# A transformer block with modulation: prologue shared out among queues and engines, row maxima of the second item spread over its own attention, last item's tail reordered

## The reference

```
c6 = silu(c) @ Wc + bc
sh_msa, sc_msa, g_msa, sh_mlp, sc_mlp, g_mlp = split(c6, 6)
xm = ln(x) * (1 + sc_msa) + sh_msa
q, k, v = xm @ Wq + bq, xm @ Wk + bk, xm @ Wv + bv
w = softmax((q / 16) . k)            # per item and head, 512 x 512
x = x + g_msa * ((w . v) @ Wo + bo)
xm2 = ln(x) * (1 + sc_mlp) + sh_mlp
x = x + g_mlp * (gelu(xm2 @ W1 + b1) @ W2 + b2)
```

## Time and profile before

| | us |
|---|---|
| median of 3 runs | 711.07 (711.01 to 713.25) |
| profiled execution, its own time | 709.01 |
| its span, first to last instruction | 707.2 |
| PE busy in it | 672.8 (95%) |
| DVE busy | 552.4 (78%) |
| ACT busy | 398.5 (56%) |
| POOL busy | 238.0 (34%) |

### The profile page before, as it was taken

The page is one execution under the profiler, slowest core; times in us unless marked ns, Lnnn a source line. Parts: engine busy times, 40 slices in busy tenths (PEclk is TensorE's granted clock), DMA queues, the critical chain, the costliest instruction groups (busy, mean ns, idle before and its releaser), DMA issues.

```text
span 707.2 us, 15832 instructions
## 1 busy us (share of the span) xinstructions
PE 672.8 (95%) x6498; PEld 410.8 (58%) x6498; DVE 552.4 (78%) x1013; ACT 398.5 (56%) x474; POOL 238.0 (34%) x179
## 2 busy tenths in 40 slices
PE   7989998989999999999999999999999989999987
PEld 6543334323787448854687448844686437833976
DVE  5989989699877988789867988789867985742654
ACT  7545663466525874288525874288625871388231
POOL 1770015103442136212452136212452213250444
PEclk9999999999999999999999999999999998999999
DMA  9745105410453007230453107230452111011110
GB/s 305 212 105 131 57 32 161 112 62 33 126 132 103 35 33 194 50 120 31 103 155 99 40 32 192 51 121 32 117 141 65 44 34 61 32 61 63 47 38 30
DMA packets 58104, 63.57 MB, mean 90 GB/s; under 512 B 7560, under 2 KB 49054, under 8 KB 58030
## 3 DMA queue, kind: packets, MB, share of 16 engines
q1 hardware_dynamic: 58032, 62.56, 30.8%
HBM read 24.15 MB, written 12.89 MB: 52 GB/s over the span
## 4 chain that ended last, share of the span: by engine, by line
PE 75%; DVE 11%; issue 4%; DMA 3%; ACT 3%; SPq 2%; POOL 1%; ACTq 0%; DVEq 0%; POOLq 0%
PE ps L821 20%; PE ps L881 13%; PE ps L767 13%; PE ps L957 12%; PE ps L827 6%; DVE mx L1222 5%; PE ps L1036 3%; PE ps L813 2%; PE ps L918 2%; SPq L491 2%; PE ps L1043 2%; ACT prob L708 1%; PE ps L926 1%; DVE stats L1143 1%; DMA qst<-mrow 1%
## 5 line engine op out<-in xcount | busy, mean ns | idle before, releaser
L1222 DVE TENSOR_REDUCE mx<-ps 128x1 f32<-128x512 f32 x512 | 330.0, 682 | 49.0 <-PE ps L827 32.7
L708 ACT ACTIVATE prob<-ps 128x1024 f32<-128x1024 f32 x256 | 248.8, 1022 | 113.7 <-PE ps L821 65.3
L821 PE MATMUL ps<-qst,kst 98*32 98x512 bf16 x1920 | 142.6, 379 | 1.7 <-ACT prob L708 1.7
L881 PE MATMUL ps<-prob,vaug 128*32 128x512 f32 x1024 | 133.7, 594 | 1.2 <-DVE mx L1222 0.5
L821 PE MATMUL ps<-kst,qst 96*32 96x512 bf16 x1348 | 127.6, 381 | 4.8 <-DVE mx L1222 3.3
L646 POOL TENSOR_TENSOR hl<-z,hh 128x512 fp32r<-128x512 f32 x64 | 82.3, 1286 | 123.1 <-DVE hh L1417 123.1
L754 ACT ACTIVATE z<-ps,bias_t 128x512 f32<-128x512 f32 x64 | 43.8, 687 | 120.7 <-PE ps L957 115.8
L821 PEld LDWEIGHTS ps<-qst,kst 98*32 98x32 bf16 x1920 | 51.9, 96 | 68.7 <-issue 25.2
L821 PEld LDWEIGHTS ps<-kst,qst 96*32 96x32 bf16 x1348 | 37.1, 94 | 82.1 <-DVE mx L1222 47.7
L767 PE MATMUL ps<-w_hi,hh 128*128 128x256 f32 x256 | 73.8, 288 | 2.5 <-POOL hl L646 2.5
L827 PE MATMUL ps<-kst,qst 96*128 96x512 bf16 x201 | 66.2, 398 | 7.3 <-DVE mx L1222 6.4
(11 more groups left out here) (144 smaller groups left out, 927.5 us busy)
## 6 DMA issues: line engine op xcount, KB each, us to landing
qst<-prob SPq DMA_DIRECT2D x72, 128.0 KB, 3.5
kst<-prob SPq DMA_DIRECT2D x72, 128.0 KB, 3.8
y_scratch<-rb SPq DMA_DIRECT2D x28, 256.0 KB, 2.0
xd<-in_x_dram SPq DMA_DIRECT2D x8, 512.0 KB, 3.9
xa<-in_x_dram SPq DMA_DIRECT2D x7, 512.0 KB, 4.6
yc<-y_scratch SPq DMA_DIRECT2D x14, 256.0 KB
rb<-r_scratch SPq DMA_DIRECT2D x14, 256.0 KB
out_dram<-xn SPq DMA_DIRECT2D x7, 512.0 KB, 3.2
```

Of the source, the lines that this page charges most:

```text
L708: act.activation(prob[:, s % 2, 2 * p:2 * p + 2, :], ps[:, 2 * p:2 * p + 2, :], ACT.Exp, scale=1.0 / DH).then_inc(exp_done, 1)
L821: m = pe.matmul(out[32 * n:32 * n + 32, :], weights[:, 32 * n:32 * n + 32], moving, start=True, stop=True, skip_group_check=True)
L881: m = pe.matmul(ps[32 * q:32 * q + 32, 4 + g % 2, :], vaug[par][:, kt, G * g + q, :], prob[:, s % 2, q, :], start=kt == 0, stop=kt == TT - ...
L1222: dve.tensor_reduce(mx[(i + 1) % 2][:, t, h:h + 1], ps[:, BANK_OF[q], :], AXX, ALU.max).then_inc(max_done, 1)
```

## The change

The edits are of three kinds.

**Prologue.** Modulation is computed turned: Wc's blocks are the weights and silu(c) moves, so the features land on partitions and `turn_modulation` goes; only the two gates are still made as rows. bc comes in with the other biases, which PE turns before the modulation. The first columns of Wc are loaded from ACT's queue, and ACT loads its exponential table before it waits for c. ACT makes the high part of Wq and Wk, POOL the low part. POOL writes the keys' rows of -1 in two pieces. For item 0, ACT makes `zh` and DVE makes `z`, from opposite banks. Three of the twelve fills of item 0's first stack are issued from ACT's queue.

**Second attention.** Of item 1's 64 blocks, 46 instead of 56 lie ahead of its attention, and 18 instead of 8 in its first steps; of item 2's, 30 instead of 40 lie in that attention and 34 instead of 24 behind it. Item 1's maxima are turned in three groups (8, 4 and 4 heads) instead of two.

**Tail.** POOL adds one half of item 7's residual and DVE the other; DVE takes the low part of hidden tile 6, POOL's inverse root no longer stands ahead of it; item 7 is normalised behind hidden tile 7; DVE and ACT share its modulation; item 6's output sum stands behind hidden tile 1 of item 7; item 7 leaves in pieces of 2, 1 and 1 token tiles.

```diff
 C_FIRST = {
     0: ((4,) * 9 + (3,) + (0,) * 6, (0,) * 9 + (1,) + (4,) * 6),
-    1: ((0, 0, 0, 0, 4, 4) + (0,) * 10, (0,) * 6 + (4,) * 10),
+    1: ((2, 1, 1, 2, 3, 3, 3, 3) + (0,) * 8, (0,) * 8 + (4, 3, 4, 3, 4, 4, 4, 4)),
 }
 REST_FIRST = {
     -1: (2, (4, 0), 3, (0, 2, 0, 2), (1, 1, 1, 1), (), (8,)),
-    0: (0, (1, 1), 3, (0, 2, 0, 2), (1, 1, 1, 1), (), (18,)),
-    1: (0, (1, 1), 0, (0, 1, 0, 1), (0, 1, 0, 1), (2, 2, 2), (3, 3, 2, 2, 2, 0, 0, 0)),
+    0: (0, (1, 1), 3, (0, 2, 0, 2), (1, 1, 1, 1), (), (8,)),
+    1: (0, (1, 1), 0, (0, 1, 0, 1), (0, 1, 0, 1), (3, 3, 3), (4, 4, 4, 4, 3, 0, 0, 0)),
 }
-ROW_ENDS = {0: (4, 8, 12, 16), 1: (8, 16)}
+ROW_ENDS = {0: (4, 8, 12, 16), 1: (8, 12, 16)}
...
@@ SP
-            for k in range(KC):
-                sp.dma_start(wc_half[k][:, 0:2 * H], Wc[k * P:(k + 1) * P, 0:2 * H]).then_inc(wc_loaded[0], 16)
...
                 elif runs(i, 2):
                     fill_stack(i + 2, 0, (0,) if i == 0 else (0, 1, 2))
                     if i != 0:
-                        fill_stack(i + 2, 1)
+                        fill_stack(i + 2, 1, (1, 2) if i == -2 else (0, 1, 2))
...
@@ POOL
+            def keys_rows(half):
+
+                pool.memset(kst[0][MROW:KROWS, 8 * half:8 * half + 8, :], -1.0).then_inc(krows_set, 1)
+                pool.wait_ge(krows_set, half + 1)
+
+            def query_weights():
+
+                w = slice(0, 2)
+                pool.wait_ge(w_split, 1)
+                pool.tensor_tensor(wqkvo[1][:, w].rearrange("p n c f -> p (n c f)"), stage[:, 0, 0:1024],
+                                   wqkvo[0][:, w].rearrange("p n c f -> p (n c f)").bitcast(F32), ALU.subtract).then_inc(w_split, 1)
...
                 if early(i) and not later(i, 2, 1):
+                    keys_rows(0)
                     norm(0, 0)
+                    query_weights()
+                    pool.wait_ge(w_split, 2)
+                    keys_rows(1)
                     value_weights()
                     norm(0, 1)
...
+                        if final(i) and j == LAST_NORM_AT:
+                            pool.wait_ge(x1_gated, i + 1)
+                            pool.wait_ge(xg_done, i + 1)
+                            pool.tensor_tensor(xa[:, 0:2, :], xa[:, 0:2, :], xd[:, 0:2, :], ALU.add).then_inc(x1_done, 1)
+                        if final(i) and j == LAST_NORM_AT + 1:
+                            norm(1, i)
+                            continue
                         pool.wait_ge(hh_done, JT * b + j + 1)
...
@@ ACT
+            for k in range(KC):
+                act.dma_start(wc_rows[k][:, 0:2 * H], Wc[k * P:(k + 1) * P, 0:2 * H]).then_inc(wc_loaded[0], 16)
...
-            act.wait_ge(const_set, 1)
-            act.activation(kst[0][MROW:KROWS, :, :], mhalf[MROW:KROWS, 0:1].unsqueeze(2).broadcast_to([KROWS - MROW, NH, S]), ACT.Copy,
-                           scale=2.0).then_inc(krows_set, 1)
+            act.wait_ge(wqkvo_loaded[0], 32)
+            act.activation(wqkvo[0][:, 0:2].rearrange("p n c f -> p (n c f)"), stage[:, 0, 0:1024], ACT.Copy).then_inc(w_split, 1)
+
+            def first_modulate():
+
+                act.wait_ge(tp_done[0], 1)
+                act.wait_ge(mod_set, 1)
+                for k in range(KC):
+                    if k:
+                        act.wait_ge(z_done[0], 1)
+                    act.activation(zh[0][:, k, :], ps[:, 2 + k, :], ACT.Identity, bias=mod[:, 2 * SH1 + k, 0:1],
+                                   scale=mod[:, 2 * SC1 + k, 0:1]).then_inc(zh_done[0], 1)
...
+                        if at(b, 0) and n == 1:
+                            act.wait_ge(part_h, 2)
+                            for slot in PART_SLOTS[1][0]:
+                                act.dma_start(kst[0][slot:MROW:NSLOT, 0:8, :], part_of(0, 1, 0)).then_inc(stack_loaded[0], 16)
...
@@ PE
+            def modulation(first, loaded):
+
+                pe.wait_ge(wc_loaded[loaded], 16 * KC)
+                for n in range(first, first + 4):
                     for k in range(KC):
-                        m = pe.matmul(ps[0:NB, MOD_BANKS[n], :], yc[:, 1, k * NB:(k + 1) * NB],
-                                      wc_half[k][:, n * 512:(n + 1) * 512], start=k == 0, stop=k == KC - 1)
+                        m = pe.matmul(ps[:, 0, 64 + n * NB:64 + (n + 1) * NB], wc_rows[k][:, n * P:(n + 1) * P], yc[:, 1, k * NB:(k + 1) * NB],
+                                      start=k == 0, stop=k == KC - 1)
+                m.then_inc(mod_turned, 1)
...
             idle(IDLE_START[0], 7)
+            pe.wait_ge(bias_loaded, 96)
+            pe.transpose(ps[:, 1, 0:BIAS_ROWS], stage[0:BIAS_ROWS, 1, 1792:1920], ident[0:BIAS_ROWS, 0:BIAS_ROWS]).then_inc(bias_turned, 1)
             pe.wait_ge(silu_done, 3)
-            modulation((0,))
-            idle(IDLE_START[1], 7)
-            turn_modulation(1, 0, 4)
...
+            modulation(2 * SH1, 0)
+            idle(IDLE_START[1] + IDLE_START[2], 7)
...
@@ DVE
             variance(0, 0)
-            add_c6(1, 0, (1,))
+            dve.wait_ge(bias_turned, 1)
+            dve.tensor_copy(bias_t[:], ps[:, 1, 0:BIAS_ROWS]).then_inc(bias_set, 1)
+            dve.wait_ge(bias_set, 1)
+            dve.tensor_scalar(bc_t[:, :, 2:4], bc_t[:, :, 2:4], 1.0, None, ALU.add).then_inc(bias_set, 1)
             for t in range(TT):
                 normalise(0, 0, xa, t)
-            set_modulation(1, 0, 4, SC1)
-            query_weights()
...
+            set_modulation(0, 2 * SH1)
+            first_modulate()
...
                         if final(i) and j == LAST_NORM_AT + 1:
+                            dve.wait_ge(hh_done, JT * b + j + 1)
+                            dve.tensor_tensor(hl[:, j % HR, :], hb[:, j % HB, :], hh[:, j % HR, :].bitcast(F32), ALU.subtract).then_inc(last_low, 1)
+                        if final(i) and j == JT - 1:
                             for t in range(TT):
                                 normalise(1, i, xa, t)
-                        if final(i) and j == JT - 1:
+                            last_modulate_second()
                             z_lo(1, i)
+                        if final(b) and j == 1:
+                            output_sum(b - 1, slice(0, TT))
```

More of the change, by code:

```diff
@@ L168 @@
 LAST_UP_BANKS, LAST_LEAD = (6, 7, 0, 1), 4
+LAST_ROWS, LAST_TILE_BANK = (slice(0, 2), slice(2, 3), slice(3, 4)), 4
 HB, HR = 2, 3
@@ L415, in modulation_rows, with load_maxima @@
             def modulation_rows():
-                sp.wait_ge(c6_added, 2)
-                sp.dma_start(c6_scr[:], stage[0:NB, 1, 256:256 + 6 * H]).then_inc(c6_written, 16)
+                sp.wait_ge(c6_added, 1)
+                sp.dma_start(gates(c6_scr), gates(stage[0:NB, 1, 256:256 + 6 * H])).then_inc(c6_written, 16)
             def step(i, par):
+                def load_maxima(b, g):
+                    first, last = group_heads(b, g)
+                    sp.wait_ge(mrow_done, 2 * rows_before(b, g) + 2)
+                    for n in range(2):
+                        sp.dma_start(qst[b % 2][MROW + n:MROW + n + 1, first:last, :], mrow[0:last - first, n, :]).then_inc(m_loaded, 16)
                 if runs(i, 2) and not early(i):
@@ L682, in modulate @@
                 for out, done in (((zh_of(n, b), zh_done[n]),) if relieved(n, b) else ()) + ((z_of(n, b), z_done[n]),):
-                    for k in range(KC):
+                    for k in range(1 if n == 1 and final(b) else KC):
                         act.activation(out[:, k, :], ps[:, banks + k, :], ACT.Identity, bias=mod[:, 2 * shift + k, bass.ds(b, 1)],
@@ L1060, in step @@
                         scores(i, par, v_blocks[t])
-                    if not later(i, 2, 1):
-                        turn_modulation(2, 4, 12)
                 else:
@@ L1446, in step @@
+                    for n in range(3 if final(b) else 1):
+                        if final(b):
+                            ts, sums = LAST_ROWS[n], ps[:, (DOWN_BANK, DOWN_BANK + 1, LAST_TILE_BANK)[n], 0:(2, 1, 1)[n] * H].unsqueeze(1)
+                        else:
+                            ts, sums = slice(0, TT), ps[:, DOWN_BANK:DOWN_BANK + 2, :]
+                        if final(b) and n < 2:
+                            dve.wait_ge(last_part, n + 1)
                         else:
                             dve.wait_ge(w2_done, JT * i)
-                        dve.tensor_tensor(osb[:, ts, :], ps[:, banks, :].rearrange("p n (t f) -> p (n t) f", t=2),
+                        if final(b) and n == 0:
+                            dve.wait_ge(out_written, 16 * b)
+                        dve.tensor_tensor(osb[:, ts, :], sums.rearrange("p n (t f) -> p (n t) f", f=H),
```

173 lines of the change are left out of this document (92 added, 81 removed).

## The result

The changed kernel took 714.42 us (median of 20 runs; 708.67 to 717.90), the kernel before 710.21 beside it (706.77 to 714.74): a ratio of 1.004, interval 1.0021 to 1.006. The profiled execution took 712.42, its span 710.6; it is one of 20, 2.0 under their median.

What follows compares the result with a forecast made beforehand. PE was taken as the bound (75% of the chain), so edits pay only where it waits. Prologue -0.9, second attention -1.2 and tail -0.9 gave -3.0 from the median 711.07: 708.1 us, range 703.5 to 711.8.

Steps and rivals of the forecast that it cites:

- The prologue: Start to DVE's first maxima: they begin at 28.45 instead of 29.35, -0.9 us, bounds +0.8 to -2.8.
- (d): Prologue: POOL fills the -1 rows in two pieces of 1.8 to 3.6 us; the second fits between 12 and 15.6.
- Part (b): Prologue: POOL's subtraction for Wq and Wk collides with DVE's normalise of item 0, ending at 12.0 to 13.1, not 11.1.
- Step (a): Prologue: bias rows, queued behind Wk, gate the modulation; rows at 8.5, normalise near 9.2, where it was or slightly ahead.
- Step (c): Prologue: ACT issues three fills, 1.9 us together, ahead of its second pair of parts, moving it from 20.34 to about 22.
- The second attention: Item 1's attention and the MLP beside it: MLP begins 5.6 us earlier, pays back 4.4; -1.2, bounds -6.8 to +1.3.
- the forecast stall for the fourth block: MLP beside the second attention: fourth block in a row waits for a bank, 0.17 us, or 0.55 behind a cast.
- case D: Second attention's new steps 0 to 3: PE waits drop its clock to half, making the kernel slower, up to 717; chance 0.08.
- The tail: Last item: PE's waits shrink and the output leaves in three pieces; -0.9 us, bounds 0 to -2.3.
- The sharing of the modulation: Tail, item 7: shared modulation saves 0.7 us, but the later normalise takes it away; 0 net.
- The output sum: Tail: moved behind hidden tile 1, it lets item 7's first cast come sooner; 0.75 of PE's 0.99 us wait.
- if the gelu is late: Tail: the lower bound of the gain, 0 us, as item 7's first cast needs the gelu too.

Runs made afterwards that it cites:

- the three pairs: Changed kernel, POOL's two instructions moved, and that with fills on SP; with against without the changed attention tables: 1.0040/0.9978, 0.9988/0.9914, 0.9982/0.9901.
- The run with the stop filled: Changed kernel, POOL's two instructions moved, fills on SP, plus 11 unused PE products ahead of the second attention: 0.9939 to the kernel before, 705.79 us.
- the run with the spread alone: Kernel before with only the changed tables of blocks and maxima for the second attention: ratio 1.0012 to the kernel before.
- the one with the wider tile: Kernel before with the turned-bias tile 8 unused columns wider: ratio 0.9972 to the kernel before.
- The best version: Changed kernel without POOL instructions beside item 0's normalise, fills back on SP, attention tables of before: 0.9901 to the kernel before, 704.59 us.

## Why the prediction was wrong

**The prologue (-0.9 forecast, +5.5 at the maxima, +7.7 at the attention).** The step that failed is (d). It gave POOL's second fill its length rightly (up to 3.6 us; 3.54) and placed it rightly (from 12; 11.48), but looked only at POOL's own queue for who would suffer. Part (b) had just told that DVE's operation waits for POOL's whole one; the fill is such a one, and two of the normalise's four operations took 2.45 and 3.68 us, where one collision and an end at 12.0 to 13.1 were counted. A second gap is in what followed: PE idle for 4.26 us and its clock at half to 21.8 us were in no term. Step (a) was right (8.5 and 9.2 forecast, 8.36 and 9.12 measured). Step (c) was right in kind: the fills on ACT moved the maxima by 1.8 (30.90 to 29.13), while the first stack's earlier landing, by which they were to pay, did not come: PE's first block behind it began at 29.51 with them and at 28.71 without. Undone together, these three bring the maxima to 28.6 to 29.5 in three traces (29.35 before): the turned and shared parts of the prologue are then worth nothing measurable there, since the stack's landing is the bound. The 2.2 us that came on top by the first attention are the clock's, as said above, and were in no term either.

**The second attention (-1.2).** In the two traces the terms were near: it began 5.5 earlier against the first (6.2 forecast), item 0's MLP 5.0 (5.6), and gave back 5.0 (4.4), which makes 0.0 of the -1.2. PE's timeline at a group of four shows the forecast stall for the fourth block, 0.29 to 0.48 us each:

```profile
203.33 0.39 PE L876 MATMUL ps<-kst,qst 96*128 96x512 bf16 x1 [0.48 <-DVE mx L1276]
```

What failed by the runs is the sign: the spread cost 4.4 to 5.8 us in the three pairs. The prediction had a mechanism for that, case D, and gave it 0.08. Four traces of the spread show it, with 10 to 14 us at 0.50; the changed kernel's own does not, so for that execution D can't be the account. The stop and the fall were in the rows of before; what was not asked is whether the clock's recovery leaned on the ten blocks that the change took from behind that stop. The run with the stop filled fits that, and no run shows it by itself.

How much of the cost is the clock's can only be estimated. Over all runs here, those of a kernel with 0.01 less mean granted clock took 4.4 us longer (a straight line through the runs within each kernel, not an experiment). The changed kernel's 20 runs had 0.979 in the mean, those of before that were timed beside the experiments 0.988: 4 us by that line. But in the three pairs the mean clocks are 0.979 and 0.982, 0.980 and 0.987, 0.981 and 0.988, with and without the spread, and by the same line that pays for 1.0 of 4.4, 2.9 of 5.3 and 3.0 of 5.8 us. Where the rest lies stays open: where the low stretch is 3.4 us long, the traces need 168.2 to 168.5 us from first to third attention with the spread and 168.1 to 168.5 without.

**The tail (-0.9; -2.26, of which some 0.7 are the tile's).** From item 6's first gelu to the end, before and the run with the spread alone have 54.3 us, the one with the wider tile 53.6, the changed kernel 52.0, the ten others with its tail 52.1 to 52.5. So the edits gave 1.1 to 1.6, and not by the term that was to give them. PE's wait of 1.29 us for a low part is gone and another came for it, much as forecast, ahead of item 7's transposes:

```profile
680.94 1.06 PE L862 MATMUL ps<-ident,xd 128*128 128x128 f32 x8 [1.33 <-DVE xd L1216]
```

The sharing of the modulation, set at 0.7 and taken as lost to a later normalise, shortened the way from the transposes to `zl` from 4.21 (675.70 to 679.91) to 2.74:

```profile
678.32 2.48 DVE L1216 TENSOR_SCALAR xd<-xa,mv,few 128x256 f32<-128x256 f32 x4
...
683.68 1.23 DVE L1290 TENSOR_TENSOR zl<-rb,zh 128x1024 fp32r<-128x1024 f32 x1
```

and the normalise came no later against the rest, though it met POOL as forecast (2.48). The output sum, set at 0.75, gave nothing: from `zl` to the first cast of item 7 there are 3.72 us, before 3.54, since the first gelu came 2.94 us behind `zl` instead of 2.19. That is the case for which the prediction had 0 as the bound ("if the gelu is late").

**The middle (nothing forecast; -2.1 in the two traces).** An item takes 79.2 and then 78.9 us, from where the tiles stand; over the five items from the third to the eighth attention that is 1.7. No edit was aimed at it and no step asked for it.

Summed by runs: POOL's two instructions with their clock cost 4.5 us (0.9978 to 0.9914), the spread 4.4 (1.004 to 0.9978), the fills at most 2; the tail gave 1.1 to 1.6, the tile 2.0 (by its interval, 4.1 to nothing). The best version is 7 us (2.4 to either side) under before; tail and tile explain some 3.4 of them. The rest was not settled: the mean granted clocks of the two are alike (0.988), so the line above gives it nothing, and in the two traces the difference is 5.2 us, of which 2.9 lie between the third attention and item 6's MLP and 2.0 in the tail.

## What to carry to other kernels

Work given to an idle GpSimd is not free if VectorE has a tensor_scalar on the path at that time (1.36 us for four of them alone, 6.69 beside two GpSimd instructions here): put both timelines beside one another and charge each GpSimd instruction, a plain fill too, with its full length. Where TensorE stops, read the granted clock two or three us later, and before blocks are moved from behind such a stop ask what TensorE will do there instead; here the unused products in the stop were worth some 3 us, and the move no gain. A trace is one execution: look at the mean granted clock of all of them before a trace is called typical. When several changes come at once, date the stages in both traces before arguing on any of them: gains and losses of 5 us stood side by side here under a difference of 3.

## What the runs showed that was not expected

A tile of 8 more unused columns, 32 bytes, made a middle item 0.33 us shorter (79.23 to 78.90): the products of 256 columns took 278 ns instead of 282 in the mean. Which of the tiles behind it matters, and why, was not tried.

A stop of PE of about 1.4 us stands ahead of the second attention in thirteen of the fourteen kernels profiled, and in twelve of them the granted clock fell to 0.50 two to three us after it began. The thirteenth, the spread alone, has the same stop (1.36 us) and no fall; in the fourteenth the stop was filled. Ahead of the first attention all fourteen have two stops of 1.2 us, and the clock fell within 3.2 us of the second one's start in seven; the kernel before is one of those without a fall, and the same instructions with the wider tile one of those with it. So such a stop makes a fall likely and does not settle it.

How long the clock then stayed low behind the stop at the second attention, 3 to 14 us, was not settled by the program either: 3 to 7 without the spread, and with it 3.4 in two traces and 10 to 14 in four, with the same waits of 0.8 and 0.9 us among the work.
